# Attention arithmetic moved from GpSimd to VectorE and TensorE in a graph-attention, linear-attention and mixture-of-experts layer

## The reference, cut to what matters

```python
def _L0_mix_ref(x, t, w_qkv, mem_kv, w_out, b_out, g_out, g_pre):
    ...
    def rmsnorm(x, g):
        n = jnp.linalg.norm(x, axis=-1, keepdims=True)
        return x / jnp.maximum(n, 1e-12) * g * x.shape[-1] ** 0.5
    xn = rmsnorm(x, g_pre)
    q, k, v = jnp.split(xn @ w_qkv, 3, axis=-1)
    ...
    q = jax.nn.softmax(q, axis=-2) * SCALE          # per head, over its 32 features
    k = jax.nn.softmax(k, axis=-1)                  # over all nodes and 4 memory slots
    context = jnp.einsum('bhdn,bhen->bhde', k, v)
    out = jnp.einsum('bhde,bhdn->bhen', context, q)
    out = rmsnorm(out @ w_out + b_out, g_out)
    return out + x
```

## Time and profile before

| what | value |
|---|---|
| median of 3 runs | 3193.95 us (3191.22 to 3210.43) |
| the profiled execution | 3190.67 us |
| its span, first to last instruction | 3188.6 us |
| busy PE / DVE / ACT / POOL | 1752.3 / 1926.5 / 1646.2 / 1847.9 us |
| mean granted TensorE clock | 0.577 of full speed |

### The profile page before, as it was taken

The page is one execution under the profiler, slowest core; times in us unless marked ns, Lnnn a source line. Parts: engine busy times, 40 slices in busy tenths (PEclk is TensorE's granted clock), DMA queues, the critical chain, the costliest instruction groups (busy, mean ns, idle before and its releaser), DMA issues.

```text
span 3188.6 us, 43599 instructions
## 1 busy us (share of the span) xinstructions
PE 1752.3 (55%) x7813; PEld 1451.3 (46%) x7814; DVE 1926.5 (60%) x3848; ACT 1646.2 (52%) x5683; POOL 1847.9 (58%) x1847
## 2 busy tenths in 40 slices
PE   4735356226555555555555555555555553468993
PEld 2415233126444444444444444444444443457872
DVE  8876879966555555555555555555555555854453
ACT  4721122147666665655555666556565563654541
POOL 0030124477777777777777777777777771334543
PEclk9866555555555555555555555555555555579997
DMA  9020000011111111111111111111111114224664
GB/s 308 0 22 4 0 0 0 3 35 29 28 28 28 28 28 29 29 29 28 28 28 29 28 29 29 28 28 28 29 28 29 29 28 120 82 83 159 193 195 134
DMA packets 148281, 161.30 MB, mean 51 GB/s; under 512 B 45795, under 2 KB 115739, under 8 KB 147938
## 3 DMA queue, kind: packets, MB, share of 16 engines
q0 software_dynamic: 60992, 82.75, 11.8%
q1 hardware_dynamic: 79856, 69.82, 7.6%
q10 hardware_dynamic: 7346, 7.78, 0.8%
HBM read 101.34 MB, written 52.35 MB: 48 GB/s over the span
## 4 chain that ended last, share of the span: by engine, by line
POOL 48%; issue 16%; DVE 16%; PE 14%; ACT 3%; DMA 1%; POOLq 0%; SPq 0%; ACTq 0%; DVEq 0%
POOL arena L1614 47%; DVE arena L658 5%; DVE arena L657 4%; PE ps L1258 3%; PE ps L1274 3%; PE ps L1148 2%; PE ps L1078 1%; PE ps L1266 1%; PE ps L1250 1%; DVE arena L675 1%; PE ps L1119 1%; POOL arena L1637 1%; PE ps L1210 1%; DVE arena L703 1%; PE ps L1222 1%
## 5 line engine op out<-in xcount | busy, mean ns | idle before, releaser
L1614 POOL DMA_INDIRECT arena<-gather_table,arena x1612 | 1526.2, 947 | 493.8 <-issue 488.8
L1182 PE MATMUL ps<-arena 128*128 x4016 | 921.3, 421 | 667.5 <-DVE big L835 667.2
L1182 PEld LDWEIGHTS ps<-arena 128*128 128x128 f32 x4016 | 875.6, 331 | 716.8 <-issue 716.7
L811 DVE TENSOR_TENSOR ps<-ps,arena 128x512 f32<-128x512 f32 x502 | 325.6, 695 | 628.5 <-ACT arena L1435 624.4
L1429 ACT ACTIVATE arena<-arena,xnx 128x2 f32 x1004 | 215.1, 285 | 744.9 <-SPq L1679 744.9
L1440 ACT ACTIVATE arena<-lane,arena 128x32 f32<-128x32 f32 x2008 | 449.4, 308 | 0.0
L824 DVE TENSOR_TENSOR arena<-ps,arena 128x1024 f32<-128x1024 f32 x251 | 307.7, 1226 | 166.2 <-ACT ps L1419 166.2
L819 DVE TENSOR_TENSOR ps<-ps,arena 128x1024 f32<-128x1024 f32 x251 | 309.3, 1232 | 63.2 <-ACT arena L1440 63.1
L1172 PE MATMUL ps<-el,pick_w 48*128 x1004 | 182.2, 287 | 242.9 <-DVE ps L811 120.5
L1418 ACT ACTIVATE arena<-ps 128x1024 f32<-128x1024 f32 x251 | 252.9, 1008 | 63.5 <-issue 62.7
L1419 ACT ACTIVATE ps<-ps 128x1024 f32<-128x1024 f32 x251 | 253.5, 1010 | 0.0
(11 more groups left out here) (286 smaller groups left out, 2240.3 us busy)
## 6 DMA issues: line engine op xcount, KB each, us to landing
arena<-gather_table,arena POOLq DMA_INDIRECT x1612, 2.4
arena<-slot_rows SPq DMA_DIRECT2D x119, 128.0 KB, 2.1
expert_rows<-arena SPq DMA_DIRECT2D x119, 128.0 KB, 2.1
slot_rows<-ends_w SPq DMA_DIRECT2D x2, 4480.0 KB, 25.6
arena<-big SPq DMA_DIRECT2D x112, 56.9 KB
slot_rows<-ends_w SPq DMA_DIRECT2D x1, 6272.0 KB, 33.6
base<-in_x_dram SPq DMA_DIRECT2D x4, 1536.0 KB, 15.3
out_dram<-base SPq DMA_DIRECT2D x5, 896.0 KB
```

What stands on the lines that cost most here:

```text
L811: ins = dve.tensor_tensor(z5[:, :, c, :, :], row, bcast(er[:, :, c, :], 3, WN), ALU.add)
L1182: ins = pe.matmul(ps[:, 6 + u % 2, i * AW:i * AW + AW], share_w[u % 4][:, (i * GT + c) * P:(i * GT + c + 1) * P], gat[:, bass.ds(place["ag ...
L1614: pool.indirect_dma_start(gat[:, p % RING, c * GW:(c + 1) * GW], None, table_d, bass.IndirectOffsetOnAxis(ap=dst_x[:, t:t + 1], axis=0)).t ...
```

## The change

GpSimd has no arithmetic of the attention left. The subtraction of the keys' maximum goes to DVE's piece (2, 3), the subtraction of the queries' maximum to (2, 5), the multiplication by the inverse sum to (5, 1). The output weight is made twice as wide: its left half is as before and serves the norm, its right half is the same times `g_out`, and the row for the bias matmul is `[b_out | b_out * g_out]`. So `mix` writes 512 columns a tile in place of 256; ACT copies the right half to `att` and squares the left half. DVE then adds the scaled row to `base` by one `scalar_tensor_tensor` a tile (49 of 128 x 256). A small tile, `memT`, moves into spare memory, and the semaphore `s_soft` goes.

```diff
-        wide_w = sb("wide_w", [P, WC + D])
+        wide_w = sb("wide_w", [P, WC + 2 * D])
-        mixw = wide_w[:, WC:WC + D]
+        mixw = wide_w[:, WC:WC + 2 * D]
...
                 if piece == (2, 3):
-                    step(dve.tensor_reduce(qst[:, 0, :], q4, AX.X, ALU.max), "qmax")
+                    for c in range(NS):
+                        kc = kv[:, TS * c:TS * c + TS, 0:HID]
+                        dve.tensor_tensor(kc, kc, bcast(kmaxb[:, :], 1, TS), ALU.subtract).then_inc(s_ksub, 1)
+                if piece == (2, 4):
+                    step(dve.tensor_reduce(qst[:, 0, :], q4, AX.X, ALU.max))
+                if piece == (2, 5):
+                    step(dve.tensor_tensor(q4, q4, bcast(qst[:, 0, :], 2, MD), ALU.subtract), "qsub")
...
-                    step(dve.reciprocal(qst[:, 1, :], qst[:, 0, :]), "qrec")
+                    step(dve.reciprocal(qst[:, 1, :], qst[:, 0, :]))
+                if piece == (5, 1):
+                    step(dve.tensor_tensor(q4, q4, bcast(qst[:, 1, :], 2, MD), ALU.mult), "qnorm")
                 if piece == (5, 2):
                     dve.wait_ge(s_once, 7)
-                    step(dve.tensor_scalar(mixw[:, :], ps[:, 5, 0:D], kmx[:, 3:4], None, ALU.mult), "mixw")
+                    step(dve.tensor_scalar(mixw[:, 0:D], ps[:, 5, 0:D], kmx[:, 3:4], None, ALU.mult))
+                    step(dve.tensor_tensor(mixw[:, D:], mixw[:, 0:D], rows_b[:, 1, :], ALU.mult))
+                    step(dve.tensor_tensor(rows_b[0:1, 1, :], rows_b[0:1, 0, :], rows_b[0:1, 1, :], ALU.mult), "mixw")
                 if level > ROWS_AT and place == 0:
...
-                    step(dve.reciprocal(tmpT[:, r], ss[:, r]), f"scale{c}")
+                    step(dve.reciprocal(tmpT[:, r], ss[:, r]))
+                    for t in range(*CHUNKS[c]):
+                        ins = dve.scalar_tensor_tensor(out=base[:, t, :], in0=att[:, t, :], scalar=tmpT[:, t:t + 1], in1=base[:, t, :], op0=ALU.mult, op1=ALU.add)
+                    ins.then_inc(s_scaled, 1)
...
-                pe.matmul(ps[:, 4 + t % 2, 0:D], qT[t % 2], mixw[:, :], start=True, stop=False)
-                pe.matmul(ps[:, 4 + t % 2, 0:D], ones[0:1, :], rows_b[0:1, 0, :], start=False, stop=True).then_inc(s_mixp, 1)
+                pe.matmul(ps[:, 4 + t % 2, :], qT[t % 2], mixw[:, :], start=True, stop=False)
+                pe.matmul(ps[:, 4 + t % 2, :], ones[0:1, :], rows_b[0:1, :, :].rearrange("p a c -> p (a c)"), start=False, stop=True).then_inc(s_mixp, 1)
...
-                        pe.wait_ge(s_soft, 2)
+                        pe.wait_ge(s_step, at["qnorm"])
...
-                act.activation(att[:, t, :], ps[:, 4 + t % 2, 0:D], ACT.Copy)
+                act.activation(att[:, t, :], ps[:, 4 + t % 2, D:2 * D], ACT.Copy)
...
-                    act.wait_ge(s_soft, 1)
+                    act.wait_ge(s_step, at["qsub"])
...
-            pool.wait_ge(s_step, at["kmaxb"])
-            for c in range(NS):
-                kc = kv[:, TS * c:TS * c + TS, 0:HID]
-                pool.tensor_tensor(kc, kc, bcast(kmaxb[:, :], 1, TS), ALU.subtract).then_inc(s_ksub, 1)
-            q4 = q_all[:, :, :].rearrange("p t (h d) -> p (t h) d", h=MH)
-            pool.wait_ge(s_step, at["qmax"])
-            pool.tensor_tensor(q4, q4, bcast(qst[:, 0, :], 2, MD), ALU.subtract).then_inc(s_soft, 1)
-            pool.wait_ge(s_step, at["qrec"])
-            pool.tensor_tensor(q4, q4, bcast(qst[:, 1, :], 2, MD), ALU.mult).then_inc(s_soft, 1)
-
-            for c, (t0, t1) in enumerate(CHUNKS):
-                pool.wait_ge(s_step, at[f"scale{c}"])
-                rows, n_ = att[:, t0:t1, :], t1 - t0
-                pool.tensor_tensor(rows, rows, bcast(tmpT[:, t0:t1], 2, D), ALU.mult).then_inc(s_scaled, 1)
-                pool.wait_ge(s_scaled, 3 * c + 1)
-                pool.tensor_tensor(rows, rows, bcast(rows_b[:, 1, :], 1, n_), ALU.mult).then_inc(s_scaled, 1)
-                pool.wait_ge(s_scaled, 3 * c + 2)
-                pool.tensor_tensor(base[:, t0:t1, :], base[:, t0:t1, :], rows, ALU.add).then_inc(s_scaled, 1)
```

More of the change, by code:

```diff
@@ L294, in gps_layer @@
         mexp = sb("mexp", [P, MEM])
-        memT = sb("memT", [MEM, 2, P])
+        memT = spare[0:MEM, T * 6:T * 6 + 2 * P].rearrange("p (a n) -> p a n", a=2)
         ctxm = sb("ctxm", [P, P])
@@ L377, in gps_layer @@
         s_mixp = sem("s_mixp")
-        s_soft = sem("s_soft")
         s_scaled = sem("s_scaled")
@@ L1409, in _ @@
             for n_, (c0, c1) in enumerate(((0, kept), (kept, T * RW))):
-                act.wait_ge(s_scaled, 3 * (len(CHUNKS) - 1 + n_))
+                act.wait_ge(s_scaled, len(CHUNKS) - 1 + n_)
                 act.activation(big[:, c0:c1], ones[:, 0:1].broadcast_to([P, c1 - c0]), ACT.Copy, scale=0.0).then_inc(s_zero, 1)
```

## The result

The changed kernel takes 3228.69 us (median of 13 runs, 3197.70 to 3240.51), the kernel before 3193.22 us (13 runs, 3187.54 to 3210.43). The ratio is 1.0079, with a 95% interval from 1.0047 to 1.0112: slower, by an amount under the 1% that was set for a difference. The medians lie 1.1% apart. The two differ because four of the thirteen runs took 3197.70 to 3204.39 us and the other nine 3226.43 to 3240.51. The four also had the higher mean granted clock: 0.583 to 0.585 against 0.575 to 0.578. The profiled execution is of the upper group: 3229.41 us, span 3227.3, against 3190.67 and 3188.6 before.

A forecast was written before the change was run, and what follows sets the result against it. The 1612 gathers follow the first, which waits for VectorE's sort. Softmax -4.2 -3.0, TensorE's chunks +18.8 +18.0 +19.4 +11.3, last chunk's VectorE -12.0: +48.3 us on 3190.67 gives 3239 us, range 3178 to 3258.

The forecast's parts named there:

- the likeliest case: Clock pattern in the row chunks stays as before: 3239 us, own range 3224 to 3250, chance 0.43.
- What bounds the kernel: 1612 gathers 1.25 us apart follow the first, which waits for VectorE's sort; moving the first moves the end equally.
- Piece 2: Level 10 of the sort: GpSimd's stall of VectorE goes, VectorE gets the subtractions; net -4.2 us.
- Piece 5: Level 13 of the sort: 10.6 us of stall go, VectorE gets qnorm and two small products; net -3.0 us.
- The price of a tile: Row chunks on TensorE: with 512 columns a tile takes 4.12 us at clock 0.50, 2.19 at 1.00.
- The slack: TensorE's idle time before the transposes behind the four chunks, 0, 3.84, 4.25 and 7.55 us, subtracted from their growth.
- The clock in the chunks: Second and third chunk fast for 6.9 us, then slow; first and last slow; growth +18.8, +18.0, +19.4, +11.3 us.
- The last chunk on VectorE: Last chunk's arithmetic: 16.4 us of stall go, eleven scale-and-adds of 0.40 us come; net -12.0 us.
- (d): Rival: the stall of VectorE isn't GpSimd's, so the moved work only adds time; 3284 us, chance 0.01.
- (b): Rival: a row chunk that has become fast stays fast to its end; +8.3 us, 3199 us, chance 0.24.
- (c): Rival: TensorE's clock is fast in every row chunk; -34.2 us, 3156 us, chance 0.10.
- (a): Rival: no row chunk has a fast stretch on TensorE; +60.3 us, 3251 us, chance 0.15.

The follow-up runs named there:

- e1_pieces: Kernel before with the softmax arithmetic of levels 10 and 13 on VectorE, GpSimd keeping the chunks; 3191.95 us against 3194.14, ratio 0.9993.
- e2_wide: Kernel before with only the matmuls widened to 512 columns, GpSimd's work all kept; 3237.56 us against 3194.14, ratio 1.0120.
- e6_tail: Kernel before with only the last chunk's arithmetic moved from GpSimd to VectorE; 3629.29 us against 3635.5, ratio 0.9987.
- c2_after: Changed kernel with only a value-preserving mask added before register waits; 3229.85 us against 3194.14 for the kernel before, ratio 1.0115.
- e7_fullrow: Changed kernel with the bias matmul given 128 rows; 3611.18 us against 3665.78 for the kernel before, ratio 0.9851.
- c3_after_again: One more execution of the kernel of c2_after, on the second chip; 3680.16 us.
- e5_both: Changed kernel without the bias matmul and with 256 columns again; 3576.16 us against 3635.5 for the kernel before, ratio 0.9835.
- e4_nobias: Changed kernel without the bias matmul, b_out/4 added to every row of the mixing weight; 3558.29 us against 3635.5 for the kernel before, ratio 0.9790.
- e3_narrow: Changed kernel with 256 columns again, VectorE multiplying by scale and g_out; 3156.95 us against 3194.14 for the kernel before, ratio 0.9880.
- e8_fullrow_before: Kernel before with the bias matmul given 128 rows, 256 columns kept; 3651.45 us against 3665.78, ratio 0.9958.

## Why the prediction was right, and where it was off

The forecast was +48.3 us; the profiled execution is 38.7 us above that of before, the medians are 35.5 us apart, and 3228.69 lies in the range and in the likeliest case's own. By its terms:

- **What bounds the kernel.** Right. Every one of the 1612 gathers moved with the first.
- **Piece 2**, forecast -4.2. The transposes of level 10 come at 232.50 instead of 234.88; `kmaxb`, which nothing of the change touches, had come 1.3 us later. The piece's own share is -3.7. **Piece 5**, forecast -3.0: between the transposes of levels 10 and 14 lie 123.77 us instead of 126.49, -2.7.
- **The price of a tile.** Right: 4.11 and 2.17 us, forecast 4.12 and 2.19. The lower bound by hidden weight loads played no part. Behind the four chunks VectorE idled for 32.89, 30.26, 36.69 and 24.01 us, over 20 for each as forecast.
- **The slack**, 0, 3.84, 4.25 and 7.55 us. Right. It was used up in all four chunks, and e1_pieces and e2_wide show both sides of it: a faster TensorE gains nothing in the narrow chunks beside GpSimd, and GpSimd's stalls cost nothing in the wide ones.
- **The clock in the chunks** is the term that was mis-sized, under "The chunks on PE", in "I keep this pattern". All four chunks had a fast stretch, not two. The growth was 15.7 + 14.8 + 19.2 + 5.4 = 55.1 us in place of 67.5. Chunk 2 was as forecast (19.4), since it had the stretch as it was forecast. Chunks 0 and 3 had two and three fast tiles more than forecast (3.1 and 5.9 us less), chunk 1 five instead of three (3.2 us less).
- **The last chunk on VectorE.** Right: the piece went from 49.37 to 37.33 us, -12.04 against -12.0, with 0.404 us a scale-and-add where 0.40 was taken; e6_tail has the same mechanism alone.

By the sum: -5.1 + 55.1 - 12.0 = +38, and the other 10 us are the clock's 12.4 less the 2.1 by which levels 10 to 14 gained less than forecast. By the chances it was a miss: slower by over 1% had 0.62, within 1% 0.29, and the ratio says 0.8%. Without the four runs near 3200 us it would have been 1.011, as in c2_after. Those four spent more time at the fast level. By an estimate from their spans and mean granted clocks (3197.7 us at 0.584 against 3227.3 at 0.578) it was some 34 us more at 1.00 and 63 us less at 0.50; fifteen tiles at 2.17 us in place of 4.11 would be 33 and 62. A chunk of 13 or 14 tiles at 1.00 to its end would give 16 to 21 us of their 25 to 30. Which chunks it was no profile shows, and why only in some executions is open.

Of the rivals, (d) fell: no comparison is stalled any more. (b) and (c) didn't come about in the changed kernel, but the mechanism of (c), which had 0.10, is real, and the reason given against it was wrong. "Unbroken work did not open it" was read from chunks in which every second matmul has one row. e7_fullrow has the longer unbroken chunks of (c) with 128 rows, and they are fast throughout: its first gather comes 54.4 us earlier than before, where (c) gave 34.2, the rest mostly the shorter tile (49 tiles by 0.36 us less than the 2.19 taken, 17.6 us). The Trainium skill (TensorE: Matmul & The Clock Gate, Part 1: The HAM clock gate) states that the gate's ratio is set by how busy TensorE has been recently. With "busy" as the profile counts it, the chunks of e7_fullrow agree (24.52 of 25.00 us busy at 0.99) and those with the one-row matmul do not: 36.50 of 36.50 us busy went at 0.50 in the changed kernel. Nor does the first half of the context pass, here in the kernel before:

```profile
249.65:267.50 17.85, 17.85 (x84) 17.85 (x85) 12.79 (x26) 4.98 (x6) 0.00 (x0) 0.50 0.00 1
```

Its matmuls have 128 rows, and every second one a single column (L1119, L1120); the second half, of the same kind, went at 0.99 in the kernel before and at 0.50 in c3_after_again. So one-row matmuls are not the only work that TensorE can be busy with at half clock.

The prediction misread one row. The clock of 0.80 from 410.00 to 411.50 does not follow transposes alone, with TensorE idle: TensorE was busy until 410.79, and the slow row chunk stood right before the transposes. Another place of the same trace shows what was meant. The 13 transposes of 325.11 come after 11.30 us of idle time, and the clock stands at 0.99 as soon as they are through, with TensorE nearly idle (a line of TensorE's timeline, and two of the busy time by stretch):

```profile
325.11 3.04 PE L1148 MATMUL ps<-ident,arena 128*128 128x128 f32 x13 [11.30 <-DVE arena L658]
...
325.10:328.20 3.10, 3.04 (x13) 2.63 (x13) 1.21 (x3) 0.63 (x2) 0.00 (x0) 0.50 0.00 0
328.60:332.00 3.40, 0.70 (x2) 0.30 (x2) 3.29 (x9) 0.02 (x1) 0.00 (x0) 0.99 0.00 0
```

Not every group of transposes is followed by a fast stretch: behind those of 234.88 the clock stayed at 0.50. But all four chunks of the changed kernel began fast, so the second case, (a), fell too.

## What to carry to other kernels

Before an elementwise operation is folded into matmul columns, read what the matmul costs at the clock that is granted there, and whether TensorE has idle time at the end of the stretch: here the fold takes 3 to 4 us a chunk off VectorE (e5_both against e4_nobias), which counted behind the last chunk only, and cost 55 us on TensorE (e2_wide). Put a bias into the weights, or give its matmul all 128 rows, rather than one row, before anything else around it is changed: that edit alone turned this change from a loss of 1.1% into a gain of 1.5% (128 rows) or 2% (in the weights), and was worth 0.4% in the kernel before, where VectorE bounds three of the chunks. And an engine's arithmetic that stalls another one is worth moving only where nothing else ends later; a table of the pieces between fixed points of the trace, one row a kernel, shows where that is.

## What the runs showed of the hardware

- **One-row matmuls and TensorE's clock.** In the eight profiled executions with the one-row bias matmul, 32 chunks, the clock stayed at 1.00 to the end in three (chunk 1 of e1_pieces, e3_narrow and e6_tail, all of 256 columns); in a fourth, chunk 3 of e3_narrow, it fell in the last tile. In the five without it, 20 chunks, it stayed in all. The context pass shows that half clock occurs without one-row matmuls too. In e7_fullrow the number of rows is all that differs in the chunks. Why these few stayed fast is open, and whether it is the rows of the stationary operand or those of the moving one is too, since the edit changes both.
- **A matmul of one row isn't cheaper.** At 1.00 a tile with it takes 2.17 us (512 columns) and 1.32 us (256); with 128 rows 1.83 and, in the mean of two, 1.07. At 256 columns, in e8_fullrow_before and in the kernel before:

```profile
435.92 0.27 PE L1091 MATMUL ps<-ident,arena 128*128 128x128 f32 x1
436.03 0.60 PE L1097 MATMUL ps<-wide_w,xnx 128*128 128x256 f32 x2
436.46 0.59 PE L1098 MATMUL ps<-rows_b,ones 128*128 128x256 f32 x2
436.89 0.27 PE L1091 MATMUL ps<-ident,arena 128*128 128x128 f32 x1
```

```profile
432.48 0.60 PE L1096 MATMUL ps<-wide_w,xnx 128*128 128x256 f32 x2
433.01 0.69 PE L1097 MATMUL ps<-rows_b,ones 1*128 1x256 f32 x2
```

- **GpSimd's stall of VectorE** is one of some instructions only: two-operand ones of 128x320 took 5.2 to 6.4 us, the reduction of 128x6272 was not held. `scalar_tensor_tensor` of 128x256, back to back, cost 0.404 us each; it was met with GpSimd idle only.
- **Chips differ in the gathers.** On the second and third chip the 1612 gathers took 2359 to 2363 and 2388 to 2389 us from the first to the last, in place of 2016, the same for every kernel on a chip to within 4 us. GpSimd waited for SyncE's queue there. In e6_tail these waits come to 365 us, in the kernel before to 1.5 us, and the gathers take 344 us longer, so they are where the time goes. The sum over all gathers, and one such wait:

```profile
L1620 POOL DMA_INDIRECT arena<-gather_table,arena x1612 | 1529.9, 949 | 881.5 <-issue 457.9 <-SPq L1685 281.8 <-SPq L1694 83.4
...
808.71 0.94 POOL L1620 DMA_INDIRECT arena<-gather_table,arena  x1 [13.24 <-SPq L1694]
```

What makes those chips' queue slower is open.
